# A twelve-layer kernel whose stages hand their semaphores back: clearing in a block of its own, or at the head of the next stage

## The reference, cut to what matters

```python
x = x + L0_xattn(_layernorm(x), ctx, ctx, mask, ...)     # 16 heads of 8
x = x + L0_attn(_layernorm(x), ...)
x = x + L0_ffn(_layernorm(x), ...)                       # 8 linear experts, soft routing
x = x + L1_xattn(_layernorm(x), ctx, ...)
x = x + L1_attn(_layernorm(x), ...)                      # rotary attention and an MLP
x = x + L1_ffn(_layernorm(x), ...)                       # top-1 of 8 experts, GELU
x = x + L2_xattn(_layernorm(x), ctx, ctx, mask, ...)
x = x + L2_attn(_layernorm(x), ...)                      # convolution and selective scan
x = x + L2_ffn(_layernorm(x), ...)                       # each expert chooses its tokens
x = x + L3_xattn(_layernorm(x), ctx, ...)                # two-way cross attention
x = x + L3_attn(_layernorm(x), ...)                      # cosine attention
x = x + L3_ffn(_layernorm(x), ...)                       # top-2 of 8 adapters, GELU
```

## Time and profile before

| | |
|---|---|
| timed runs | 3711.79 us median, 3706.45 to 3715.58 |
| span of the profiled execution | 3723.7 us |
| instructions | 79487 |
| granted TensorE clock, mean | 0.905 |
| stretches between the release of a block's barrier and that of the clearing block behind it | 52 |

### The profile page before, as it was taken

The page is one execution under the profiler, slowest core; times in us unless marked ns, Lnnn a source line. Parts: engine busy times, 40 slices in busy tenths (PEclk is TensorE's granted clock), DMA queues, the critical chain, the costliest instruction groups (busy, mean ns, idle before and its releaser), DMA issues. The chain is left out here.

```text
span 3723.7 us, 79487 instructions
## 1 busy us (share of the span) xinstructions
PE 3048.7 (82%) x23799; PEld 2074.7 (56%) x23799; DVE 2475.2 (66%) x6665; ACT 2021.1 (54%) x6297; POOL 1888.7 (51%) x2012
## 2 busy tenths in 40 slices
PE   6989697879999898695999996878771768969967
PEld 5769534446666685463777762333341437736645
DVE  7976676558888673444888886898976123457863
ACT  5545405558888554233777765454530125558954
POOL 4640203457777792072666656888850531117830
PEclk9999799989999899797999998999985888878979
DMA  3310002322222000111111113444440229800000
GB/s 104 86 32 0 6 1 66 97 69 79 80 81 79 8 2 6 60 48 46 37 37 37 37 38 120 137 137 142 136 148 4 33 43 250 183 7 1 2 7 23
DMA packets 142433, 233.68 MB, mean 63 GB/s; under 512 B 28796, under 2 KB 104862, under 8 KB 141575
## 3 DMA queue, kind: packets, MB, share of 16 engines
q1 hardware_dynamic: 134088, 221.61, 20.7%
q0 software_dynamic: 8128, 9.45, 1.4%
HBM read 200.44 MB, written 13.71 MB: 58 GB/s over the span
## 5 line engine op out<-in xcount | busy, mean ns | idle before, releaser
L3223 PE MATMUL l2a_pY<-l2a_hc,ident 128*128 128x512 f32 x512 | 275.2, 677 | 89.8 <-POOL l2a_hc L3142 55.3
L2461 POOL TENSOR_TENSOR l2x_att_prob<-l2x_att_prob,l2x_att_rs 128x1024 f32<-128x1024 f32 x128 | 242.6, 1895 | 144.5 <-DVE l2x_att_rs L2692 144.5
L3112 POOL TENSOR_TENSOR l2a_dbu<-l2a_dx,l2a_BC 128x1024 f32<-128x1024 f32 x128 | 298.7, 2355 | 21.2 <-PE l2a_pY L3223 10.6
L2461 POOL TENSOR_TENSOR l1x_att_prob<-l1x_att_prob,l1x_att_rs 128x1024 f32<-128x1024 f32 x128 | 242.5, 1895 | 107.4 <-DVE l1x_att_rs L2692 107.4
L2649 ACT ACTIVATE l2x_att_prob<-l2x_att_pS,l2x_att_nmx 128x257 f32<-128x257 f32 x512 | 236.3, 475 | 92.1 <-DVE l2x_att_nmx L2687 92.1
L3240 ACT ACTIVATE l2a_pA<-l2a_dl,l2a_A 128x512 f32<-128x512 f32 x256 | 174.5, 689 | 187.9 <-DVE l2a_pH L3346 112.2
L2649 ACT ACTIVATE l1x_att_prob<-l1x_att_pS,l1x_att_nmx 128x257 f32<-128x257 f32 x512 | 236.4, 475 | 73.4 <-DVE l1x_att_nmx L2687 73.3
L3223 PEld LDWEIGHTS l2a_pY<-l2a_hc,ident 128*128 128x128 f32 x512 | 103.6, 211 | 253.0 <-issue 120.5
L2687 DVE TENSOR_REDUCE l1x_att_nmx<-l1x_att_pS 128x1 f32<-128x257 f32 x512 | 181.9, 418 | 88.2 <-PE l1x_att_pS L2560 88.2
L3346 DVE TENSOR_TENSOR_SCAN l2a_pH<-l2a_pA,l2a_dbu 128x512 f32<-128x512 f32 x192 | 224.8, 1217 | 23.4 <-POOL l2a_dbu L3112 11.9
L2687 DVE TENSOR_REDUCE l2x_att_nmx<-l2x_att_pS 128x1 f32<-128x257 f32 x512 | 182.0, 418 | 49.9 <-PE l2x_att_pS L2565 49.9
(11 more groups left out here) (766 smaller groups left out, 9099.3 us busy)
## 6 DMA issues: line engine op xcount, KB each, us to landing
l2a_BC<-l2a_rows SPq DMA_DIRECT2D x128, 512.0 KB, 3.7
l3x_att_ctn<-ctx_n SPq DMA_DIRECT2D x32, 576.0 KB, 13.6
l0x_att_kvs<-ctx_t SPq DMA_DIRECT2D x32, 514.0 KB, 3.5
l1x_k_xin<-ctx_t SPq DMA_DIRECT2D x32, 514.0 KB, 3.5
l1x_att_ctx<-ctx_t SPq DMA_DIRECT2D x128, 128.5 KB, 2.1
l1x_att_kT<-l1x_KA SPq DMA_DIRECT2D x128, 128.5 KB, 2.2
l2x_att_ctx<-ctx_t SPq DMA_DIRECT2D x128, 128.5 KB, 2.1
l3x_att_ctx<-ctx_t SPq DMA_DIRECT2D x32, 514.0 KB, 11.5
```

Source lines behind the costliest of these rows:

```text
L2461: pool.tensor_tensor(p, p, bc(rs[:, b, :], 2, LAST), ALU.mult).then_inc(scaled, 1)
L3112: pool.tensor_tensor(dbu[:, u % 3], dx[:, g % 2], bc(BC[:, u % RING, 0, :], 1, NC), ALU.mult).then_inc(dbu_made, 1)
L3223: last = pe.matmul(pY[c][:, :], env.ident[:, :], hc[:, u % 3, c, :], start=False, stop=n == NS - 1)
```

## The change

The clearing block of a stage is left out. An ended stage puts its semaphore numbers on a list, `ENDED`, and keeps the semaphores held. The next stage that calls `open` adds its ones first, `opened` last, as before; then GpSimd clears the numbers of all stages on the list, with the same instruction, and goes on with its own work. The numbers are released for new use only when that later stage has ended. What is on the list at the end of the program is cleared in one last block.

```diff
 def stage(nc, title):
     with ExitStack() as ctx:
-        sems, primed = [], []
-        opened = ctx.enter_context(nc.semaphore(f"{title}_opened"))
+        sems, primed, cleared, held = [], [], [], ExitStack()
+        opened = held.enter_context(nc.semaphore(f"{title}_opened"))
         sems.append(opened)
 
         def sem(name):
-            sems.append(ctx.enter_context(nc.semaphore(f"{title}_{name}")))
+            sems.append(held.enter_context(nc.semaphore(f"{title}_{name}")))
             return sems[-1]
+
+        def open_(pool):
+            for s in primed + [opened]:
+                pool.sem_inc(s, 1)
+            while ENDED:
+                cleared.append(ENDED.pop())
+                clear(pool, cleared[-1][0])
...
-            open=lambda pool: [pool.sem_inc(s, 1) for s in primed + [opened]],
+            open=open_,
             opened=opened,
         )
-        numbers = sorted(s.num for s in sems)
-        starts = [k for k in numbers if k - 1 not in numbers]
-        ends = [k + 1 for k in numbers if k + 1 not in numbers]
-        with nc.Block() as block:
-            @block.gpsimd
-            def _(pool):
-                for low, high in zip(starts, ends):
-                    pool.sem_clear(range(low, high))
+        ENDED.append(([s.num for s in sems], held))
+        for _, free in cleared:
+            free.close()
+
+ENDED = []
+
+def clear(pool, numbers):
+    starts = sorted(k for k in numbers if k - 1 not in numbers)
+    ends = sorted(k + 1 for k in numbers if k + 1 not in numbers)
+    for low, high in zip(starts, ends):
+        pool.sem_clear(range(low, high))
...
         for layer in LAYERS:
             layer(nc, env, a)
+    with nc.Block() as block:
+        @block.gpsimd
+        def _(pool):
+            for numbers, _ in ENDED:
+                clear(pool, numbers)
+    while ENDED:
+        ENDED.pop()[1].close()
```

More of the change, by code:

```diff
@@ L3918, in build @@
 def build(nc, a, out):
+    ENDED.clear()
     with ExitStack() as ctx:
```

## The result

The changed kernel took 3687.7 us (median of 6 runs, 3677.9 to 3700.25), the kernel before 3710.32 us on the same chip (6 runs, 3704.57 to 3715.58). The ratio is 0.9937, with a 95% interval of 0.9921 to 0.9953: 22.6 us, or 0.6%. The forecast was 3685.6 us. The profiled execution's span is 3692.2 us, against 3723.7 before.

A forecast was written before the change was run, and what follows sets the result against it. Taken to bound the kernel: a chain of stages, with idle seams at barriers wholly on the path. 26.75 us removed less 0.5 added gives 26.2 us; from the median 3711.8 that forecasts 3685.6 us, range 3676 to 3699.

The forecast's parts named there:

- What bounds the kernel: Between stages all five engines meet in a barrier; 52 stretches without work, 27.71 us in sum, lie on the path.
- What is removed: At the seams, 49 stretches go whole (25.98 us) and the program's end gives 0.77 us: together 26.75 us.
- the 49 stretches: All stretches between two releases but the last three of the 52; they go as a whole, 25.98 us.
- the end: The program's last three stretches, 1.73 us, become one block of about eight clears at 0.96 us, gaining 0.77 us.
- the split into parts: Each stretch was split into 0.24 us for drains and second barrier plus 0.09 us of GpSimd's queue per clear.
- the rival of a barrier that stays: If a barrier remained at each seam, only clears would move: 11.8 us stay, 3697 us; chance 0.01.
- What is added: Clears in GpSimd's queue at stage heads, on the path only where others wait for GpSimd's first result: 0.5 us.
- three heads: Starts of l0's and l1's block attentions and l1's experts, where others wait for GpSimd: five clears, say 0.5 us.
- X coming back: Around 3028 us, four loads of X might land too late for VectorE; costed at nothing, at most 0.85 us lost.
- Code blocks: Loops at L2372 might fetch code on each of 60 returns: 18 to 36 us back, up to 3722 us; chance 0.03.
- GpSimd's heads: Clears on the path in most stages, in twice the runs: 14.0 to 27.9 us back, 3699.6 to 3713.5; chance 0.06.
- TensorE's clock: Matmul groups caught at the lower clock, five more or fewer being 8 us: 3677.5 to 3693.7 us; larger swing's chance 0.04.

The follow-up runs named there:

- the first two experiments: The changed kernel with one empty block (barrier) at each of the 52 stage ends, 3701.5 us; then with four at each, 3764.2 us.
- The first experiment: The changed kernel with one empty block, barrier and all, at each of the 52 stage ends: 3701.5 us, ratio 0.9985 to the kernel before.

## Why the prediction was right

**What bounds the kernel.** The seams, with no engine at work, were on the path whole. Shown twice over: taking them away gave 0.66% on average over five measurements (24 us), and 52 and 208 barriers put back cost 18 and some 80 us by the times (19 and 72 us in the profiles).

**What is removed.** 26.75 us were forecast, 26.90 came: 25.98 for the 49 stretches, as read, and 0.92 instead of 0.77 us for the end, whose block had six clears and not eight (0.81 us, not 0.96). The sum was safe because it took whole stretches as read and not the split into parts. That split was mis-sized: the barrier is 0.33 and not 0.24 us, because one clear hides under the drains, and a stretch also depends on which clears it has (0.33 or 0.39 us with one). It fed only the end block, the first two experiments and the rival of a barrier that stays, whose 3697 us should have been 3702. The first experiment, close to that case, measured 3701.5 us; by its ratio of 0.9985 that is 3706 us beside the 3711.8 of the forecast.

**What is added.** 0.5 us were forecast for three heads. Against the release ScalarE starts 0.16 us later in l0's block attention (4.05 to 4.21), 0.26 in l1's (4.05 to 4.31), and l1's first gather 0.09 later (0.86 to 0.95): 0.51 us. The numbers didn't break up: 152 clears. In l3's attention 16 clears wait together instead of 13; GpSimd starts 1.2 us later there, at 2.84 us behind the release, and TensorE starts, still after the load, at 5.05 as before (5.11). The nine-fold clears show how thin some covers are: l3's attention has a margin for its 16, not for 144.

**X coming back** cost nothing: VectorE reads X 0.05 us behind the release in both kernels.

**The rivals.** *Code blocks*: between the first and the last of the 30 returns of each loop no code is loaded in any of three profiles of the changed kernel, and the kernel isn't slower. But the mechanism is real in another place. I had looked for fetches on a loop's return and overlooked the plain case: a fetch in straight code that falls on a small awaited load. It takes back 1.1 us in l1's list stage and 1.2 us or more in l2's, 2.3 of the 26.9 us. The Trainium skill (Runtime: NRT & Kernel Launch, section Instruction fetch mechanics) calls the fetch of the next 16 KiB block mostly hidden. For the engine that executes the code the trace agrees in the main: in l3's cross projection one profile of the kernel before has a packet of q8 1.05 us behind the release and the other none, and TensorE's busy time is 20.84 us in both; the 0.30 us at 1716.08 are an exception. The fetch isn't hidden from others: one such packet, 1.16 us long, beside loads of 20 KB and 0.5 KB. *GpSimd's heads*: didn't come; 0.5 us instead of 14 or more. *TensorE's clock*: this rival was read too simply. The prediction took the clock for scatter. Part of it is: l3's query projection moves by 9 us and the span of one program from 3682 to 3697 us, in both kernels alike. But part of it goes with the kernel: -5.7 us in l0's experts, +1.7 in l3's cross projection, and, in the mean of two profiles before and five after, +2.7 in l0's attention and +2.5 in l2's cross attention.

The whole: -26.9 for the stretches, +0.5 for the three heads, +2.3 for the code fetches is -24.1 us, a ratio of 0.9935 against the mean of 0.9934 measured. So close an agreement is luck. The sum leaves out every stage that repeats at another clock. Over two profiles of the kernel before and five of the changed program, twelve stages differ by 0.3 us or more in their means with no overlap between the kernels, from -5.7 to +2.7 us. Together, the two list stages included, they come to +1.1 us, so they nearly cancel, which nothing in the prediction foresaw. What the seams cost is shown; that the rest comes to almost nothing is not explained.

## What to carry to other kernels

Cut the span at the releases of the barriers and ask each stretch what work it holds; where the answer is none, its whole length can be had, however small each is (0.33 us times 52 was most of this). Bookkeeping that is moved into an engine's queue should stand behind whatever wakes the others and ahead of something that is waited for anyway; which heads have such cover is read from who ends their idle time. Before a stage is blamed for having become slower, look at its granted clock and at a second profile of each kernel: l3's query projection changed as much without any edit, l0's experts kept a time and a clock of their own in each kernel.

## What the hardware showed that I had not expected

A barrier of five engines takes 0.33 us, with one short semaphore clear in it or with none; most clears back to back start 0.07 us apart.

Untouched work can run at another clock, and do so every time: 192 matmuls of l0's experts keep TensorE busy for 84.5 us in both profiles of the kernel before and for 78.4 us in all five of the changed program.

The position of one engine's code decides the speed of another engine's loads: 46 drains on TensorE at the start of the program, 1500 us earlier, shortened a stage that waits for SyncE's loads to 23.83 us. It takes 24.85 us with 46 drains on SyncE itself, and 24.49 to 25.12 us in the five profiles of the changed program without either.

GpSimd's memset of 1.8 us and VectorE's casts hold each other up. With nine-fold clears ahead of it the memset started beside a cast of 4096 elements (L1770) and took 3.15 us. In the changed kernel a cast of a 1x128 row (L1767) that starts beside it takes 1.79 us, and takes 0.22 us in the version in which the memset has run before:

```profile
27.28 1.79 DVE L1767 CAST l0x_att_pick_b<-ones 1x128 bf16<-1x128 f32 x1
```

```profile
27.38 0.22 DVE L1767 CAST l0x_att_pick_b<-ones 1x128 bf16<-1x128 f32 x1
```
